# A two-stage expert layer around a recurrence: logits products of 128 columns, and a new plan

## Chip, cores and metric

One Trainium2 chip, one of its cores. The metric is the device time of one execution in microseconds, the median of the runs. All arithmetic is 32-bit floating point. A matrix product of this type is issued as two passes of TensorE, each with its own load of the stationary operand. The counts in the views are of such passes.

## What is computed

The reference, cut to its core, on 16 sequences of 512 tokens of 128 channels:

```python
def ffn(x, router_w, fc, proj):            # 8 experts, hidden width 512
    expert = argmax(softmax(x @ router_w.T))        # one expert for each token
    h = square(relu(x @ fc[expert]))
    return h @ proj[expert].T
x = x + 0.5 * ffn(layernorm(x))
x = x + rnn(layernorm(x))        # h = tanh(x @ Wi.T + bi + h @ Wh.T + bh), 512 steps
x = x + 0.5 * ffn(layernorm(x))
```

The 512 steps of the recurrence are one after the other. All 16 sequences move together, so a step's product moves 16 columns.

## The kernel before, in words

**Units, routes, tiles.** Time is cut into 16 units of 32 steps. A unit is 512 tokens, that is four blocks of 128 rows. A layer of experts handles its tokens in *routes*. The first layer has three, of 4, 4 and 8 units (FIRST, line 25), the second has seven (SECOND, line 28). For a route the kernel decides each token's expert. Blocks are transposed (`turn`), multiplied with the router's weights (`logits`, lines 1637 to 1647), the largest logit is taken (`pick`), a prefix count over the tokens gives each one's rank within its expert (`rank`), and `place` turns that into a row of a DRAM buffer sorted by expert. GpSimd (POOL in the views) then scatters the route's normalised rows, one indirect DMA for each block of 128. `head` and `entry` (first layer) or `list` (second) work out which sorted rows make a *tile*. A tile is 128 rows of one expert: 85 tiles in the first layer, 71 in the second.

**Stages.** A tile of the first layer may hold tokens of several units. A route's tile list is cut into stages (STEP, line 26, in units). Unit u of a route is complete when the tiles up to the end of its stage plus 7 more (one less than the experts) are stored (`needed`, lines 78 to 80). Route 1 (units 4 to 7) has STEP 3. Its first stage ends after 12 blocks, so unit 4 is complete with its 19th tile. Then POOL gathers the unit's four blocks back (`gather`, line 1197), VectorE (DVE) adds them, the unit is normalised (for a group of MIDDLE, line 27, together), transposed and multiplied with Wi, and its 32 steps can run.

**Beats.** TensorE (PE), VectorE and ScalarE (ACT) work in beats of one tile each. In a beat the next tile is transposed (`turn_x`, line 1684), the present one gets its first product (`product1`, 8 passes, line 1695), the one before its second (`product2`, 8 passes, line 1705). DVE does the relu of the present tile (line 1375) and finishes the last (lines 1382, 1385). ACT squares (line 1513) and copies the next tile's expert weights (line 1504), whose place it reads from the loaded tile. Some four steps of the recurrence (line 1715) lie between the products. Smaller pieces (decisions, statistics, transposes, logits) are put into beats as well. On DVE they come behind the relu and the finish (`b.dve`), or ahead of the relu (`b.front`). In the kernel before, `front` is only for the work of a recurrence unit that is soon due (`hurry`, line 713).

**Who sets the order.** Each engine's queue is an order written out ahead by `plan` (lines 147 to 810), a planner in Python. It plays all engines forward with constants for every duration and picks by urgency, with weights from PR (line 42). It has a model of TensorE's clock in `matmuls` (lines 367 to 379). Where the clock would fall it can put in idle products (`fill`, lines 404 to 409, emitted by `warm_up`, line 1722), in the kernel before only until the first tile is ordered. `keep_warm` (line 1718) issues two passes of 256 columns, in a beat that has steps but no tile.

**Queues.** POOL does the scatters (lines 1178, 1183), the gathers (1197), the output scatters of the second layer (`put`, 1203) and the reciprocal roots. Between indirect DMAs that come close together the planner puts a `rest`, a memset of 600 columns (line 1166), so that they follow each other at PACE 1.75 us. The sync engine's queue (SP) does the loads of tiles in order (line 1067 in the second layer) and the stores. A tile's load waits until the buffer of 12 tiles before is free, which in the second layer means that tile's put has landed. When the last route is counted, SP writes eight blank tiles behind the experts' rows (`close`, line 1080). The last 18 of the 71 tiles can be loaded only behind the last unit's four scatters.

**Start.** `first_in` (lines 127 to 139) orders the input loads: rows of units 0 to 3, zeros of the first buffer, then the rows of units 4 to 7 around the projection and fc weights, by AHEAD (line 50).

The product in question:

```python
j = 4 * i + q
mm = pe.matmul(lg[:, j * E:(j + 1) * E], xrt[:, m % XRING, q * P:(q + 1) * P], rwT, start=True, stop=True)
```

## Time and profile before

| | |
|---|---|
| median of 3 runs | 580.89 us (580.31 to 581.51) |
| profiled execution | 578.79 us |
| its span, first to last instruction | 576.4 us |
| mean granted TensorE clock | 0.950 |
| busy: PE, PE weight loads | 532.8 us (92%), 520.4 us (90%) |
| busy: DVE, ACT, POOL | 405.9 us, 315.4 us, 450.0 us |
| idle memsets on POOL (line 1166) | 141.8 us, 229 of them |

The profiled execution took 2.1 us less than the median, and 2.4 us of it lie outside the span. Busy shares are averages over stages with different limits, so the time is read by stage: a start up to the first tile's load, a stretch of tiles alone, the recurrence with tiles between its steps, and a tail behind the last step. A granted clock of 1.00 is 2.4 GHz, 0.50 is 1.2 GHz. DVE durations that overlap by some 0.1 us belong to a pipeline.

### The profile page before, as it was taken

How to read it: one execution, taken by the hardware profiler on the slowest of the kernel's cores; microseconds unless marked ns; L12 is line 12 of the kernel's file. 1: busy time of each engine (PE TensorE's matmuls, PEld its weight loads, DVE VectorE, ACT ScalarE, POOL GpSimd, SP SyncE). 2: the span in 40 equal slices, each digit the busy share in tenths (PEclk: the TensorE clock that was granted, in tenths of full speed). 3: DMA queues.
4: the chain of work that ended last, by engine and by line, in shares of the span. 5: the costliest groups of instructions: out<-in, count | busy, mean ns of one | idle time of the engine just before them, and what ended most of it. 6: DMA issues, size and time to landing. Idle time of an engine off the chain costs nothing.

```text
span 576.4 us, 15923 instructions
## 1 busy us (share of the span) xinstructions
PE 532.8 (92%) x4541; PEld 520.4 (90%) x4541; DVE 405.9 (70%) x1485; ACT 315.4 (55%) x1104; POOL 450.0 (78%) x562
## 2 busy tenths in 40 slices
PE   6849998899999999999999999999999999988991
PEld 6848997899999999999999999999999999877991
DVE  4799486778686798697569865777586467784650
ACT  2222363556666666566665666666656665544560
POOL 2497887559898887088997989978998938899982
PEclk8666599999999999999999999999999999999996
DMA  7974822222222232133323333322332301435410
GB/s 246 274 267 167 253 89 69 74 67 74 75 68 86 73 79 62 39 93 108 93 65 79 106 110 100 91 61 75 93 103 80 108 20 70 144 125 143 115 40 0
DMA packets 54147, 58.88 MB, mean 102 GB/s; under 512 B 8983, under 2 KB 42018, under 8 KB 54064
## 3 DMA queue, kind: packets, MB, share of 16 engines
q1 hardware_dynamic: 43776, 36.15, 21.4%
q0 software_dynamic: 9440, 21.06, 11.6%
q8 instruction: 40, 0.66, 0.5%
q10 hardware_dynamic: 848, 0.66, 0.5%
q14 instruction: 43, 0.35, 0.2%
HBM read 27.67 MB, written 30.62 MB: 101 GB/s over the span
## 4 chain that ended last, share of the span: by engine, by line
PE 71%; POOL 8%; DVE 8%; issue 5%; DMA 3%; SPq 1%; ACT 1%; POOLq 0%; ACTq 0%; DVEq 0%
PE yp L1705 23%; PE hp L1695 22%; PE z L1715 11%; PE mT L1601 4%; PE xTp L1684 4%; POOL idle L1166 3%; POOL xy_dram L1183 3%; PE lg L1645 3%; PE z L1665 2%; POOL out_dram L1203 2%; DMA hsT<-in_L_attn_x_dram 2%; ACT s_sb L1513 1%; PE hp L1720 1%; DVE pay L1252 1%; DVE r_sb L1375 1%
## 5 line engine op out<-in xcount | busy, mean ns | idle before, releaser
L1705 PE MATMUL yp<-projT,s_sb 128*128 x1248 | 204.0, 292 | 8.5 <-ACT s_sb L1513 8.2
L1695 PE MATMUL hp<-xT_sb,w_sb 128*128 128x128 f32 x1248 | 200.7, 289 | 0.3 <-ACT w_sb L1504 0.2
L1705 PEld LDWEIGHTS yp<-projT,s_sb 128*128 128x128 f32 x1248 | 164.1, 193 | 10.9 <-issue 10.8
L1695 PEld LDWEIGHTS hp<-xT_sb,w_sb 128*128 128x128 f32 x1248 | 166.0, 196 | 1.7 <-issue 0.5
L1484 ACT ACTIVATE hsT<-z 128x16 f32<-128x16 f32 x512 | 93.7, 183 | 134.1 <-PE z L1715 124.4
L1715 PE MATMUL z<-hsT,wT 128*128 128x16 f32 x1024 | 156.7, 229 | 0.1
L1715 PEld LDWEIGHTS z<-hsT,wT 128*128 128x128 f32 x1024 | 153.7, 190 | 3.2 <-ACT hsT L1484 0.3
L1513 ACT ACTIVATE s_sb<-r_sb 128x256 f32<-128x256 f32 (+1 forms) x260 | 114.2, 452 | 63.0 <-DVE r_sb L1375 31.6
L1375 DVE TENSOR_SCALAR r_sb<-hp 128x512 f32<-128x512 f32 x156 | 106.9, 685 | 56.9 <-PE hp L1695 54.8
L1166 POOL MEMSET idle<- 128x600 f32 x229 | 141.8, 619 | 0.2
L1504 ACT ACTIVATE w_sb<-fc_sb 128x256 f32 (+1 forms) x259 | 112.8, 455 | 4.6 <-issue 2.2
L1197 POOL DMA_INDIRECT back<-xy_dram,pos x64 | 62.9, 983 | 45.5 <-issue 37.9
L1203 POOL DMA_INDIRECT out_dram<-y_sb,xs_sb x71 | 70.7, 996 | 23.7 <-issue 14.0
L1183 POOL DMA_INDIRECT xy_dram<-pay,pos x64 | 63.3, 988 | 21.2 <-issue 10.2
L1178 POOL DMA_INDIRECT xs_dram<-pay,pos x64 | 62.9, 983 | 13.3 <-issue 10.4
L1369 DVE COPY xT_sb<-xTp 128x128 f32<-128x128 f32 x143 | 43.9, 307 | 12.8 <-PE xTp L1684 10.8
L1684 PE MATMUL xTp<-ident,xs_sb 128*128 128x128 f32 x156 | 47.0, 301 | 5.7 <-DVE xT_sb L1369 3.1
L1385 DVE TENSOR_SCALAR y_sb<-yp 128x128 f32<-128x128 f32 x85 | 24.5, 288 | 31.9 <-PE yp L1705 31.2
L1382 DVE SCALAR_TENSOR_TENSOR y_sb<-yp,xs_sb 128x128 f32<-128x128 f32 x71 | 20.6, 290 | 34.8 <-PE yp L1705 32.8
L1252 DVE TENSOR_SCALAR pay<-pay,mv,rstd 128x128 f32<-128x128 f32 x128 | 44.6, 488 | 0.4 <-POOL rstd L1156 0.4
L1645 PE MATMUL lg<-wT,xrt 128*128 128x8 f32 x256 | 41.0, 279 | 0.6 <-DVE pos L1298 0.3
L1156 POOL TENSOR_TENSOR rstd<-veps,half 128x4 f32<-128x4 f32 (+4 forms) x23 | 39.9, 1734 | 1.9
(133 smaller groups left out, 502.4 us busy)
## 6 DMA issues: line engine op xcount, KB each, us to landing
xs_sb<-xs_dram SPq DMA_DIRECT2D x71, 129.0 KB, 2.2
xy_dram<-zeros SPq DMA_DIRECT2D x11, 512.0 KB, 5.1
xs_sb<-xy_dram SPq DMA_DIRECT2D x85, 64.0 KB, 1.9
xy_dram<-y_sb SPq DMA_DIRECT2D x85, 64.0 KB, 1.6
hsT<-in_L_attn_x_dram SPq DMA_DIRECT2D x14, 256.0 KB
hsT<-n_L_ffn_expert_proj_dram SPq DMA_DIRECT2D x2, 1024.0 KB, 16.3
fc_sb<-in_L_ffn_expert_fc_dram SPq DMA_DIRECT2D x1, 2048.0 KB
out_dram<-y_sb,xs_sb POOLq DMA_INDIRECT x71, 2.6
```

What stands on the lines that cost most here:

```text
L1166: pool.memset(idle[:, :], 0.0).then_inc(s_idle, 1)
L1178: pool.indirect_dma_start(out=xs2_dram, in_=pay[:, n, :], in_offset=None, out_offset=bass.IndirectOffsetOnAxis(ap=pos[:, 1, n:n + 1].bitca ...
L1183: pool.indirect_dma_start(out=xy1_dram[r.index], in_=pay[:, n, XN:XN + D], in_offset=None, out_offset=bass.IndirectOffsetOnAxis(ap=pos[:, ...
L1203: pool.indirect_dma_start(out=out.rearrange("b t d -> (b t) d"), in_=y_sb[:, g % RING, :], in_offset=None, out_offset=bass.IndirectOffsetO ...
L1375: dve.tensor_scalar(r_sb[:, g % 2, :], hp[:, g % 2, :], 0.0, None, ALU.max).then_inc(s_relu, 1)
L1484: act.activation(state(t), z_step(t), ACT.Tanh).then_inc(s_h, 1)
L1504: act.activation(w_sb[:, g % 2, half * w:(half + n) * w], fc_sb[:, bass.ds(offsets[g] + half * w, n * w)], ACT.Copy).then_inc(s_wst, n)
L1513: act.activation(s_sb[:, g % 2, half * w:(half + n) * w, :].rearrange("p c t -> p (c t)"), r_sb[:, g % 2, half * w * P:(half + n) * w * P] ...
L1684: pe.transpose(xTp[:, 0:P], xs_sb[:, g % RING, XN:XN + D], ident[:, :]).then_inc(s_tx, 1)
L1695: mm = pe.matmul(hp[:, g % 2, h * P:(h + 1) * P], w_sb[:, g % 2, h * P:(h + 1) * P], xT_sb[:, g % 2, :], start=True, stop=True)
L1705: mm = pe.matmul(yp[:, 0:D], s_sb[:, g % 2, h, :], projT[:, bass.ds(offsets[g] + h * D, D)], start=(h == 0), stop=(h == HC - 1))
L1715: pe.matmul(z_step(t), WhT, state(t - 1) if t else hsT[:, 0:B], start=False, stop=True, skip_group_check=True).then_inc(s_mm, 1)
```

## The change

Six things are edited.

1. **Logits.** The router's weights get 120 columns of zeros behind their 8, set by one more memset on POOL. Each logits product moves 128 columns (fewer where the bank ends) and writes its 8 logits and zeros behind them, which the next product overwrites.
2. **The planner's clock.** Its model counts moved columns alone. Logits count as 128. `fill` works until the first tile's beats, measured from the end of PE's last real work (`worked`).
3. **The last route's decisions** may go to `front`, ahead of the relu.
4. **The puts.** None is planned from the last route's pick (less 2.011 us) until its scatters are ordered (`keep`), and behind them puts have no rests.
5. **Sizes.** Route 1 has STEP 2, so its first stage ends after 8 blocks and unit 4 is complete with its 15th tile. Units 11 to 14 are grouped as 1 and 3, where they were 2 and 2 with neighbours. Of the input rows, unit 6 is loaded earlier and unit 7 later, behind fc.
6. **PR.** New values throughout, so the order on every engine is new.

```diff
-STEP = [1, 3, 1]
-MIDDLE = [1, 1, 1, 1, 1, 1, 1, 1, 1, 2, 2, 2, 1]
+STEP = [1, 2, 1]
+MIDDLE = [1, 1, 1, 1, 1, 1, 1, 1, 1, 2, 1, 3, 1]
...
-AHEAD = [2, 4, 7]
+AHEAD = [3, 3, 6]
...
-            p = min((p for p in pool_wait if p[0] <= start), key=pool_urgency)
+            if ("pick", second[-1]) in ev and second[-1] not in sorted_out:
+                soon = [p for p in pool_wait if p[1][0] != "put" or max(pool_free, p[0]) < ev["pick", second[-1]] + PR["keep"]]
+                start = max(pool_free, min([p[0] for p in soon], default=limit))
+                if start >= limit:
+                    return
+            else:
+                soon = pool_wait
+            p = min((p for p in soon if p[0] <= start), key=pool_urgency)
...
-                while REST and drained > start + PR["burst"]:
+                while REST and drained > start + PR["burst"] and not (what == "put" and second[-1] in sorted_out):
...
-                clock = 0.5 if moved < 12 and clock == 1.0 else 1.0 if busy > 0.95 * WINDOW else clock
-                begun, busy, moved = begun + WINDOW, 0.0, 0.0
+                clock = 0.5 if moved < ACTIVE else 1.0
+                begun, moved = begun + WINDOW, 0.0
...
-                n = int((need[0] - pe) / 0.25) if not order else 0
+                n = int((max(need[0], pe) - worked) / 0.25) if len(order) <= 1 else 0
                 if n > 0:
                     b.idle[place] = n
+                    pe = worked
                     matmuls(2 * n, 128, 0.0)
...
-                hurry = isinstance(job[0], Middle) and (job[0].u0 * UNIT - t) * 0.66 < PR["crit"]
+                hurry = (job[0].u0 * UNIT - t) * 0.66 < PR["crit"] if isinstance(job[0], Middle) else job[0] and job[0].second and job[0].last and PR["end"] > 0
...
-        wT = sb("wT", [P, 2 * P + E])
+        wT = sb("wT", [P, 3 * P])
...
+            pool.memset(wT[:, 2 * P + E:], 0.0).then_inc(s_const, 1)
...
                 for q in (2 * half, 2 * half + 1):
-                    j = 4 * i + q
-                    mm = pe.matmul(lg[:, j * E:(j + 1) * E], xrt[:, m % XRING, q * P:(q + 1) * P], rwT, start=True, stop=True)
+                    at = (4 * i + q) * E
+                    n = min(P, 512 - at)
+                    mm = pe.matmul(lg[:, at:at + n], xrt[:, m % XRING, q * P:(q + 1) * P], wT[:, 2 * P:2 * P + n], start=True, stop=True)
```

## Rows read from the trace of the kernel before

**Rows 1.** The page, part 2: busy tenths and granted clock in 40 slices.

```profile
PE   6849998899999999999999999999999999988991
...
PEclk8666599999999999999999999999999999999996
```

**Rows 2.** The chain that ended last, in order of time: start, length, what.

```profile
54.23 1.78 DMA xs_sb<-xy_dram
```

**Rows 3.** Stretches of PE: length, busy (passes), granted clock, DMA share, GB/s.

```profile
49.00:52.00 3.00, 3.00 (x16) 0.50 0.47 167
...
56.00:72.13 16.13, 15.83 (x74) 0.50 0.79 250
```

**Rows 4.** PE's groups in 49 to 55 us, then in 20.7 to 24.3 us.

```profile
L1645 PE MATMUL lg<-wT,xrt 128*128 128x8 f32 x22 | 4.9, 348 | 0.0
L1601 PE MATMUL mT<-ident,hsT 128*128 128x128 f32 x8 | 2.2, 429 | 0.0
...
L1725 PE MATMUL yp<-ident 128*128 128x128 f32 x8 | 1.9, 421 | 0.0
```

**Rows 5.** Timeline of PE: last logits before the first tile; later two beats' second products.

```profile
53.42 1.71 PE L1645 MATMUL lg<-wT,xrt 128*128 128x8 f32 x8
...
542.96 1.06 PE L1705 MATMUL yp<-projT,s_sb 128*128 x8
...
544.85 1.06 PE L1705 MATMUL yp<-projT,s_sb 128*128 x8
```

**Rows 6.** Timeline of the start: route 0's logits, normalisation, pick, first scatter; route 1's rank.

```profile
14.30 3.42 PE L1645 MATMUL lg<-wT,xrt 128*128 128x8 f32 x16
...
16.88 1.12 DVE L1252 TENSOR_SCALAR pay<-hsT,mv,rstd 128x128 f32<-128x128 f32 x4 [3.51 <-POOL rstd L1156]
17.91 0.28 DVE L1259 TENSOR_REDUCE best<-lg 128x16 f32<-128x128 f32 x1
...
24.13 1.23 POOL L1183 DMA_INDIRECT xy_dram<-pay,pos  x1 [7.29 <-DVE pos L1298]
...
41.57 0.29 PE L1653 MATMUL lg<-oh,before 128*128 128x128 bf16 x1 [7.96 <-DVE oh L1263]
```

**Rows 7.** The steps as a whole; unit 4's last tile, its gather, the steps around.

```profile
L1715 PE MATMUL z<-hsT,wT x1024: 179/262/283, 116.7 to 495.7; 128*128 128x16 f32 x171
...
191.76 0.29 DVE L1385 TENSOR_SCALAR y_sb<-yp 128x128 f32<-128x128 f32 x1
...
194.92 1.00 POOL L1197 DMA_INDIRECT back<-xy_dram,pos  x1 [1.70 <-issue]
...
207.48 0.29 PE L1715 MATMUL z<-hsT,wT 128*128 128x16 f32 x2
...
215.80 0.29 PE L1715 MATMUL z<-hsT,wT 128*128 128x16 f32 x2
```

**Rows 8.** keep_warm's stretch (L1720 alone), then all engines: PE, PEld, DVE, ACT, POOL.

```profile
485.00:497.00 12.00, 6.61 (x20) 3.07 (x20) 1.00 0.35 105
...
497.00:523.00 26.00, 20.98 (x179) 19.85 (x177) 18.72 (x64) 12.66 (x24) 23.55 (x30) 1.00 0.45 134
523.00:533.00 10.00, 8.87 (x74) 8.46 (x75) 4.88 (x13) 5.13 (x9) 9.01 (x12) 1.00 0.53 147
```

**Rows 9.** Timeline of the last unit's decision: DVE, then POOL.

```profile
506.02 0.18 DVE L1259 TENSOR_REDUCE best<-lg 128x4 f32<-128x32 f32 x1
...
510.63 0.29 DVE L1298 TENSOR_SCALAR pos<-posf 128x4 int32<-128x4 f32 x1
...
511.05 0.97 POOL L1203 DMA_INDIRECT out_dram<-y_sb,xs_sb  x1 [0.17 <-issue]
...
512.80 0.97 POOL L1178 DMA_INDIRECT xs_dram<-pay,pos  x1 [0.17 <-issue]
```

**Rows 10.** Timeline of the end: DVE's last result, POOL's last put.

```profile
564.79 0.29 DVE L1382 SCALAR_TENSOR_TENSOR y_sb<-yp,xs_sb 128x128 f32<-128x128 f32 x1 [1.50 <-PE yp L1705]
...
565.88 0.97 POOL L1203 DMA_INDIRECT out_dram<-y_sb,xs_sb  x1 [0.20 <-issue]
```

More of the change, by code:

```diff
@@ L41 @@
 JMAX = UR * max(FIRST + MIDDLE + SECOND)
[L42 to L47 removed]
+PR = {'proj': -47.746, 'lat1': 14.303, 'lat2': 5.889, 'lat3': -50.516, 'last': -221.946,
+      'hor': 129.448, 'beat': 9.17, 'put': -26.524, 'dve': 2.201, 'act': 2.925, 'pe': 2.195,
+      'early': 0.409, 'load': 2.441, 'hold': -40.798, 'slack': 191.806, 'near': 0.051,
+      'tol': 0.107, 'mix': -11.014, 'late': 6.755, 'root': -17.056, 'gather': -114.978,
+      'scatter1': -67.157, 'scatter2': 5.337, 'crit': 18.341, 'front': 7.019, 'dvx': 0.781,
+      'burst': 0.3, 'keep': -2.011, 'end': 1.531}
 TURNS = ("turn", "turn2", "hadd")
 EARLY = 8
[L50 removed]
+AHEAD = [3, 3, 6]
 FORCED = ("x", "b0", "c0", "d0")
@@ L214, in plan @@
     turns_of, logits_of, est, held = [], [], {}, []
-    clock, begun, busy, moved = 1.0, 0.0, 0.0, 0.0
+    clock, begun, moved, worked = 1.0, 0.0, 0.0, 5.0
     def ahead_of(r):
@@ L367, in matmuls @@
     def matmuls(n, columns, need):
-        nonlocal pe, clock, begun, busy, moved
+        nonlocal pe, clock, begun, moved, worked
         at = max(pe, need)
@@ L427, in split @@
                 if p[0] == "logits":
[L428 removed]
+                    return passes(place, 4, 128, (("turn", p[1], p[2]), lg_after[p[1].index]), p if half else None)
                 return passes(place, 4, 128, (("turn2", p[1]), ("h", UNIT * (p[1] - 1) - 1) if p[1] >= 2 else None), p if half else None)
```

20 lines of the change are left out of this document (7 added, 13 removed).

## The prediction

> **What bounds the kernel now.** I read the page's slices first, then the chain, then each stretch by itself. TensorE is busy in nearly every slice from the second sixth to the end, but its granted clock is low in slices 2 to 5 [rows 1]. So two things cost time: stretches in which PE works at 1.2 GHz, and the few in which it idles. The chain names where the first tile comes from: its load lands at about 56.0 us [rows 2]. Ahead of that PE's clock costs little, because the wait is for route 0's scatters. From there to 72.13 PE is busy 15.83 of 16.13 us at clock 0.50 [rows 3]. That stretch is on the path: behind it tiles and steps queue for PE until the last tile. At full clock a beat of a tile alone takes 544.85 - 542.96 = 1.89 us for 17 passes, 0.111 us each [rows 5]. In the slow stretch a pass takes 15.83 / 74 = 0.214 us [rows 3].
>
> The recurrence runs from 116.7 to 495.7 us [rows 7], 0.742 us a step over 511 intervals, with PE full in the slices [rows 1]. So it shares a bound with the tiles. Only at two places does one stand without the other: no step starts for 8.32 us at unit 4 [rows 7], while tiles run on, and in 485 to 497 us there is no tile to go with the steps and keep_warm runs idle products [rows 8]. In the tail PE idles 26.00 - 20.98 = 5.0 us up to 523 and 1.1 us up to 533 [rows 8]. Then beats follow at 1.89 us to the end.
>
> **The parts of the change.** *Wider logits, their direct price.* In the low clock the 22 logits passes and 8 transposes of 128 columns fill 49 to 55 us, and the mean durations differ by 429 - 348 = 81 ns [rows 4]. That is their length, not their spacing: of 49 to 52 us they take 3.00 for 16 passes, 0.19 us each, against 0.214 in the stretch that is mostly 128 columns [rows 3]. The price is between 0 and 0.03 us a pass at low clock. It is nearest 0, because the weight loads are unchanged. At full clock a 128-column pass takes 0.111 us [rows 5], and no row times a run of 8-column ones, so the bound is 0.111 at most for each of the 128 passes after 72 us (half of 256), 14 us. I take 0, since a step's 16-column pass is 262 ns long in the median against 1.06 us for eight 128-column ones that still start 0.111 apart [rows 5, 7]: the width hides in the pipeline. A gain from width alone is excluded, since nothing is left out.
>
> *Wider logits, the clock.* In 49 to 52 us PE is 3.00 of 3.00 us busy and the clock is 0.50 [rows 3]. Three quarters of the passes are 8 columns wide [rows 4]. The clock was back at 24.3 us behind a stretch with eight idle products of the identity and transposes [rows 1, 4]. So busy time is not what lifts it. Moved columns fit, and columns that are nearly all zero (the identity's) seem to count. With 128 columns for each logits pass I expect full clock from about 43 us on, and `fill` to hold it over the 0.9 us before 56.0. The 74 passes then need 74 x 0.111 = 8.2 us, not 15.83: 7.6 less. Half of the shorter stretch's pieces hang on DVE and ACT. If PE idles there as much as in the tail's 26 us, 5.0 of 26 [rows 8], the stretch lasts 8.2 / 0.81 = 10.1 and 5.7 are gained. I take 7.0. The ends are 0 and 7.9 (with the 0.3 of idle).
>
> A rule of the Trainium skill speaks against this part. "TensorE: Matmul & The Clock Gate", Part 1, says that the clock depends on how busy the engine has been, and gives full clock after a sustained busy stretch. By that rule wider logits change nothing. Rows 3 do not agree: fully busy, and 0.50.
>
> *The start.* Route 0's last 16 logits passes take 3.42 us from 14.30, and its pick starts at 17.91, its first scatter at 24.13 [rows 6]. At full clock these passes take 1.8 us. Then the pick could start 1.6 us sooner. DVE's normalisation stands from 16.88 to 18.00 [rows 6], and the new order can put it behind. The bound is 0 to 2.5 us (another 0.9 if the rank's passes, too, run at full clock). I take 1.5. POOL's added memset stands ahead of the constants that PE and DVE wait for: under 0.62 us by the 600-column memset of the table, 0.1 taken, inside this term. Unit 7's rows come behind fc now. What covers it is DVE: PE waited 7.96 us for DVE's pick of route 1, not for rows [rows 6]. If that cover went, route 1's scatters would be late, and next its tiles, which are due only when route 0's 23 are done.
>
> *STEP 2.* The gather of unit 4 starts at 194.92, 3.16 us behind the 19th tile's result at 191.76 [rows 7]. Four tiles fewer, each in a beat of some four steps (4 x 0.742 = 3.0 us), put it some 12 us sooner, and more than the stall is covered. The recurrence gains 8.32 - 0.74 = 7.6 us. PE does not, because it worked on tiles there. POOL has four gathers to do inside route 2's scatters, so these end 4 x 1.75 = 7.0 us later: late next would be route 2's first tiles. The regrouped units change no count of roots or pieces, and one DVE instruction of `place` goes: 0.
>
> *What the freed recurrence is worth.* With the last step 7.6 sooner, keep_warm's stretch goes. Its 20 passes of 256 columns are worth some 20 x 0.22 = 4.4 us of tiles. The tail's 6.1 us of idle shrink if more tiles are left to cover the last decision. Together 10.5 us at most, 0 at least; below zero if the new order makes idle of its own, as much as the tail's 5.0. I take 4.5, under half, since POOL is 78% busy, and nearly full in the late slices' rows (23.55 of 26 us) [rows 8], so it gives no free hand.
>
> *The last decision.* Its pick starts at 506.02 behind a relu and a finish, its positions end at 510.92, but POOL is in a put from 511.05 and scatters at 512.80 [rows 9]. Ahead of the relu the pick can start up to 1.7 us sooner, and without the put the scatter starts 1.75 sooner. This lies on the recurrence's path: steps, decision, scatter, last 18 tiles. PE's own path is the longer one as long as it has tiles, so I count 0.5. Bounds are -1 and 3.4. The negative end is a held put: its buffer is waited for by the load 12 tiles on, that load stands ahead of the rest on SP, and PE waits for it.
>
> *No rests in the tail.* The last result is ready at 565.08, and the last put starts at 565.88, behind a rest [rows 10]. It could start at 565.25: 0.6 us. Before that tiles come at 1.89 us, slower than the pace of 1.75, so rests cost nothing else.
>
> Sum: 7.0 + 1.5 + 4.5 + 0.5 + 0.6 = 14.1 us. From the profiled execution's 578.8 that gives 564.7. The median lay 2.1 higher, so 566.8. I say 566.5.
>
> **The rivals.** *All idle recovered.* The plan was written for a clock that the chip did not grant from 43 to 72 us. One that is right there may also remove the small stalls: 7.9 + 2.5 + 10.5 + 1 + 0.6 = 22.5, so 558.4. For it speaks that PE is the only bound in most slices. Against it stands POOL's load.
>
> *Only the clock's part.* PE gains 7 us and the new order loses what it recovers: 580.9 - 7.0 - 0.6 = 573.3. For it speaks that idle in the tail comes from DVE and SP chains that a sum of PE time does not show.
>
> *Columns don't set the clock.* Something else in these passes keeps it low, or zeros don't count. Then the change does not do what it says, and only the plan's parts remain: 580.9 - 4.5 - 0.6 = 575.8. This is also what the busy-time rule above would give. Rows 3 and 4 speak against it.
>
> *Slower: fill at half clock.* The place is the wait for the first tile. PE's real work ended there at about 55.1 [rows 5]. A plan that believes in full clock has it end near 50 and puts (56.0 - 50) / 0.25 = 24 idle products, 48 passes, behind it. At 0.50 they last 48 x 0.214 = 10.3 us from 55.1, to 65.4: the first tile is 9.4 late. The rest gains 0.6 and perhaps 3: 580.9 + 9.4 - 3.6 = 586.7. It decides from the point where the clock at 50 us is 0.50 and idle passes number more than (0.9 + 3.6) / 0.214 = 21. The clock's fall and rise in slices 2 to 5 [rows 1] speak for it a little. The identity's columns speak against it.
>
> **Chances.** My forecast (562 to 571) 0.52, all recovered 0.20, clock alone 0.16, columns don't count 0.05, slower by fill 0.04, no change at all 0.03. The likeliest case's time is the prediction, 566.5. The range takes in the first three cases and most of their bounds: 556 to 576. A measurement of this kernel can tell about 0.2% (1.2 us) from no change. Faster by more has 0.93, within it 0.03, slower 0.04.
>
> **What would show it.** Clock 1.00 from about 43 to 72 us, and the first tile's beats at about 1.9 us from 56. First scatter at 22 to 23 us. The first step at 107 to 110, and no gap of several us at step 128. Fewer than 20 idle passes of 256 columns. PE's idle between the last step and the last scatter's load below 5 us. The last put 0.2 us behind the last result. It would be wrong if the clock is 0.50 at 60 us with 128-column logits, if a new gap stands in the steps at unit 8 or later (route 2's tiles late), or if the tail's idle grows.

## The result, and the profile after

The changed kernel is slower by about half a percent. Over 16 runs its median is 583.29 us, against 581.31 us for 16 runs of the kernel before beside it; the ratio is 1.0053, 95% interval [1.0028, 1.0078]. A second set on another chip gave 1.0078 [1.0041, 1.0114]. The forecast was 566.5 us in a range of 556 to 576. The granted clock differs from execution to execution: fourteen of the changed kernel's runs go from 580.3 us at a mean clock of 0.988 to 588.1 at 0.971, and two slow ones, which no ratio counts, took 592.1 and 594.6 us at 0.961 and 0.958. So single profiles are compared by their parts, and the ratios carry the verdicts.

The page of the changed kernel, part 2, against [rows 1], and its stretches of PE against [rows 3] (length, busy and passes, clock, DMA share, GB/s):

```profile
PE   7899988899899999999999999999999999769991
...
PEclk9999999999999999999999999999999999979997
```

```profile
49.00:52.00 3.00, 3.00 (x28) 1.00 0.60 225
56.00:72.13 16.13, 15.03 (x123) 1.00 0.76 230
```

The clock is at 1.00 through the whole start, where it was 0.50 in both stretches. In the same 3 us PE gets 28 passes done instead of 16. In the other row, besides a fuller third slice, two slices near the end are at 7 and 6 tenths where there were 9 and 8.

The start, on GpSimd (first scatters of route 0), and the last logits before the first tile, against [rows 5, 6]:

```profile
20.13 1.24 POOL L1193 DMA_INDIRECT xy_dram<-pay,pos  x1 [3.60 <-DVE pos L1308]
...
32.22 0.96 POOL L1193 DMA_INDIRECT xy_dram<-pay,pos  x1 [5.60 <-DVE pay L1262]
```

```profile
54.66 2.01 PE L1657 MATMUL lg<-wT,xrt 128*128 128x128 f32 x16
56.50 1.50 PE L1737 MATMUL yp<-ident 128*128 128x128 f32 x12
```

The first scatter is 4.0 us earlier than in [rows 6], and the gain is gone twelve us later: the fifth scatter waits 5.60 us for VectorE's normalised rows and starts at 32.22, where it started at 31.40 before.

The steps (TensorE's instructions of the recurrence, first and last start), and the steps around unit 4, against [rows 7]:

```profile
L1727 PE MATMUL z<-hsT,wT x1024: 182/262/374, 114.1 to 492.6; 128*128 128x16 f32 x171
```

```profile
208.23 0.29 PE L1727 MATMUL z<-hsT,wT 128*128 128x16 f32 x2
212.57 0.29 PE L1727 MATMUL z<-hsT,wT 128*128 128x16 f32 x2
```

The stall at unit 4 is 4.34 us instead of 8.32, yet the last step is only some 3 us earlier.

The stretch from the last step on, all engines (PE, PEld, DVE, ACT, POOL), against [rows 8]:

```profile
497.00:523.00 26.00, 17.40 (x122) 16.43 (x123) 13.58 (x47) 9.12 (x18) 19.79 (x23) 0.87 0.41 115
523.00:533.00 10.00, 10.00 (x92) 10.00 (x91) 6.01 (x16) 5.76 (x10) 4.93 (x6) 1.00 0.54 146
```

PE idles 8.6 of the first 26 us instead of 5.0, and does 122 passes instead of 179, because the clock also falls: it is 0.50 from 506.5 to 509.9 and from 513.3 to 516.7. Here the time went. GpSimd, then VectorE and one row of ScalarE in that stretch, against [rows 9] (only the rows that matter; "remote" is a count that arrived later than any record of the work that raises it):

```profile
499.64 1.00 POOL L1213 DMA_INDIRECT out_dram<-y_sb,xs_sb  x1 [0.30 <-issue]
500.94 0.99 POOL L1213 DMA_INDIRECT out_dram<-y_sb,xs_sb  x1 [0.30 <-issue]
...
508.10 0.99 POOL L1188 DMA_INDIRECT xs_dram<-pay,pos  x1 [0.35 <-issue]
...
514.66 1.00 POOL L1213 DMA_INDIRECT out_dram<-y_sb,xs_sb  x1 [0.30 <-issue]
515.96 0.99 POOL L1213 DMA_INDIRECT out_dram<-y_sb,xs_sb  x1 [0.30 <-issue]
```

```profile
505.48 0.29 DVE L1392 SCALAR_TENSOR_TENSOR y_sb<-yp,xs_sb 128x128 f32<-128x128 f32 x1 [1.80 <-remote]
505.59 0.28 ACT L1530 ACTIVATE xT_sb<-xTp 128x128 f32<-128x128 f32 x1 [1.19 <-remote]
506.56 0.56 DVE L1308 TENSOR_SCALAR pos<-posf 128x4 int32<-128x4 f32 x1
...
520.59 0.29 DVE L1392 SCALAR_TENSOR_TENSOR y_sb<-yp,xs_sb 128x128 f32<-128x128 f32 x1 [3.88 <-remote]
```

The last decision is indeed earlier: scatters from 508.10, against 512.80. But puts stand 1.30 us apart on both sides of it, and VectorE twice waits for TensorE's semaphores, although the matmuls that raise them (yp from 500.68, in 8 passes of 0.11 us) are long recorded as done. VectorE's instruction at 520.59 also waits for the put of the tile 12 before it, whose output buffer it reuses, but that put's count had stood since 470.9 us. In the trace's records of the semaphores only TensorE's counts are late. Four pieces of its work, recorded as ended at 501.74, 501.95, 502.11 and 503.04 us, are counted at 505.46, 505.53, 505.56 and 505.65. Most counts come 0.01 us behind the recorded end. The last of the four has eight passes of 0.11 us in it, 0.9 us of work, and its count stands 0.09 us behind the one before. So this work had been done, and its counts came late. For the first of the four alone that is not settled.

The end, against [rows 10]:

```profile
567.78 0.29 DVE L1392 SCALAR_TENSOR_TENSOR y_sb<-yp,xs_sb 128x128 f32<-128x128 f32 x1 [1.49 <-PE yp L1717]
```

```profile
568.88 0.98 POOL L1213 DMA_INDIRECT out_dram<-y_sb,xs_sb  x1 [0.55 <-issue]
```

The last result is 2.99 us later than before, and the last put still stands 1.10 us behind it (start to start), without a rest.

**One table for all runs.** I cut each profiled execution at two events: the first step and the last step (ScalarE's tanh), and measured on to VectorE's last result. The three lengths sum to the time of the last result.

| kernel | first step | steps | last step to last result |
|---|---|---|---|
| before | 117.0 | 379.3 | 68.4 |
| changed | 114.5 | 378.5 | 74.9 |
| changed, second profile (e20) | 114.5 | 377.1 | 75.3 |
| e1 wide logits alone | 113.1 | 381.1 | 69.6 |
| e2 change, rests back | 114.3 | 381.2 | 71.0 |
| e3 change, decision behind relu | 115.3 | 378.1 | 76.3 |
| e5 before, no rests past the last scatter | 111.4 | 380.5 | 73.2 |
| e6 change, old constants | 114.7 | 392.7 | 68.7 |
| e7 e2 with idle passes at tile 37 | 114.4 | 382.2 | 71.5 |
| e8 e2 with the list behind relu | 113.3 | 377.8 | 72.6 |
| e10 change, rests back ahead only | 115.1 | 379.9 | 76.0 |
| e11 change, short rests | 113.4 | 376.7 | 69.9 |
| e12 e1, places early | 112.6 | 380.4 | 69.7 |
| e13 e1, 12 scatters bare | 111.9 | 378.8 | 68.2 |
| e14 change, rests back behind only | 113.4 | 384.3 | 69.9 |
| e15 e1, all scatters bare | 109.0 | 378.0 | 68.7 |
| e16 e1, puts bare in the middle | 112.5 | 379.3 | 70.7 |
| e17 e1, five puts bare | 113.0 | 381.0 | 69.0 |
| e18 e1, no rests past the last scatter | 111.1 | 381.4 | 73.9 |
| e19 e5 again | 113.9 | 381.0 | 73.4 |

Before, e5 and e19 run one program up to the last scatter, and their first steps lie at 117.0, 111.4 and 113.9. So a difference of 3 us in the first column of two single profiles shows nothing. Nor is the clock at the start the same in the three. The half-clock stretch that ends at 72.1 us in the kernel before ends at 61.8 in e5 and at 62.1 in e19. Their rows for the stretch that [rows 3] give with 74 passes at 0.50 (e5, then e19):

```profile
56.00:72.13 16.13, 16.05 (x117) 0.82 0.88 266
56.00:72.13 16.13, 16.04 (x114) 0.81 0.85 262
```

The third column sets the change off clearly: 74.9 and 75.3 against 68.4. It has its own scatter, from execution to execution and chip to chip. Five profiles have before's tail unchanged (before, e1, e13, e15, e16) and go from 68.2 to 70.7, mean 69.1. The same tail without rests behind the last scatter (e5, e18, e19) has 73.2 to 73.9, mean 73.5. The change's tail with rests behind the last scatter (e2, e7, e11, e14) has 69.9 to 71.5, mean 70.6, and without them (the change twice, e10) 74.9 to 76.0, mean 75.4. So the rests are worth 4.4 and 4.8 us of this column, beyond the scatter. The change's order costs 1.5 and 1.9 on the means, which is within it or near.

### The profile page after: what moved, and what is told of

Its sections match the earlier page's. It is cut to its first block, busy times and chain, and to the rows that moved or that the text cites. A ratio compares the mean times of both kernels' runs of the same rounds, so it can differ in the third digit from the quotient of the medians.

```text
span 579.0 us, 16141 instructions
## 1 busy us (share of the span) xinstructions
PE 536.5 (93%) x4665; PEld 522.6 (90%) x4665; DVE 403.6 (70%) x1474; ACT 318.2 (55%) x1111; POOL 434.9 (75%) x538
## 4 chain that ended last, share of the span: by engine, by line
PE 71%; DVE 11%; issue 5%; POOL 4%; DMA 3%; SPq 2%; another core or an unknown queue 1%; ACT 0%; POOLq 0%; ACTq 0%; DVEq 0%
PE yp L1717 24%; PE hp L1707 22%; PE z L1727 12%; PE mT L1611 4%; PE xTp L1696 4%; PE z L1677 3%; PE lg L1657 3%; POOL xy_dram L1193 2%; DVE pay L1262 2%; DMA hsT<-in_L_attn_x_dram 1%; POOL idle L1176 1%; DVE r_sb L1385 1%; DVE stats L1252 1%; SPq L1046 1%
## 5 line engine op out<-in xcount | busy, mean ns | idle before, releaser
L1176 POOL MEMSET idle<- 128x600 f32 x204 | 126.7, 621 | 0.4
L1514 ACT ACTIVATE w_sb<-fc_sb 128x256 f32 (+1 forms) x257 | 113.1, 458 | 4.6 <-issue 1.6
L1379 DVE COPY xT_sb<-xTp 128x128 f32<-128x128 f32 x133 | 39.6, 298 | 9.6 <-PE xTp L1696 5.4
L1262 DVE TENSOR_SCALAR pay<-pay,mv,rstd 128x128 f32<-128x128 f32 x128 | 45.9, 509 | 0.0
L1657 PE MATMUL lg<-wT,xrt 128*128 128x128 f32 x256 | 38.5, 285 | 0.2 <-ACT xrt L1544 0.2
```

What stands on the lines that cost most here:

```text
L1176: pool.memset(idle[:, :], 0.0).then_inc(s_idle, 1)
L1514: act.activation(w_sb[:, g % 2, half * w:(half + n) * w], fc_sb[:, bass.ds(offsets[g] + half * w, n * w)], ACT.Copy).then_inc(s_wst, n)
```

## The experiments

All ratios are against the kernel before on the same chip. The experiments ran in five groups, each on a chip of its own: e1 to e5, e6 to e10, e11 to e14, e15 to e17, e18 to e20. So medians in us are compared within a group only, and ratios of different groups with both intervals.

**e1: the wide logits alone.**

```
 before
-    mm = pe.matmul(lg[:, j*E:(j+1)*E], xrt[...], rwT, ...)
+    at = (4 * i + q) * E
+    n = min(P, 512 - at)
+    mm = pe.matmul(lg[:, at:at + n], xrt[...], wT[:, 2*P:2*P + n], ...)
 (and the zeros of wT with the counts of s_const)
```

> The kernel before with one part of the change alone: the logits' products are 128 columns wide (the zeros of the weight tile and their memset with them); plan, order, rests and decisions stay as before. Theory A (the columns set the clock, and the step pipeline turns the clock into time): granted clock 1.00 in most of 0 to 75 us and mean clock above 0.97, first y some 5 us earlier, and the end 3 to 8 us earlier than before (573 to 578 against 581). Theory B (the early lead is lost later whatever the plan, because loads, GpSimd and the routes' stalls set the middle and the tail): the same clock and first y, but the end within 1.5 us of before. Theory C (the columns do not set the clock): clock 0.50 for 16 of the first 72 us as before, and no change.

Measured: ratio 0.9970 [0.9946, 0.9994], 577.69 us against 579.76. Its page and its stretches:

```profile
PEclk9878999899999999999999999999999999999996
```

```profile
49.00:52.00 3.00, 3.00 (x28) 1.00 0.46 169
56.00:72.13 16.13, 16.04 (x124) 0.89 0.88 264
```

The width of the logits does change the clock: beside one memset nothing else changed, and the clock at 49 to 52 us is 1.00, in all six profiles with this start, against 0.50 in all three with narrow logits. The mean clock is 0.973 against 0.954. But the end comes only 2.1 us earlier (of a forecast term of 7.0), between theories A and B. Its six profiles (e1, e12, e13, e16 to e18, all with this start) have the first step at 111.1 to 113.1, mean 112.4; the three with narrow logits have a mean of 114.1. The first tile is finished at 64.2 instead of 68.5, but e5 and e19, with narrow logits, finish it at 64.9. Against them the lead is 0.7 us, and PE does 124 passes from 56.00 to 72.13 where they do 117 and 114. So most of the term of 7.0 us was the long half-clock stretch of one execution. In the two others PE did 28 and 29 passes at 0.50 from 56.0 to 61.8 us, 5.8 us that would take 3.1 to 3.2 at 0.111 us a pass. That leaves an estimate of 2.6 to 2.7 us to gain, near e1's 2.1.

**e2, e3: the tail of the changed kernel, rests and decision.**

```
 e2: change
+ from 16 entries ahead of the last scatter on: one rest ahead of each put
+ that follows a put or a scatter; several rests in a row become one
 e3: change
+ for b in beats:
+     late = [p for p in b.front if len(p) > 1 and getattr(p[1], "last", False)]
+     b.front = [p for p in b.front if p not in late]
+     b.dve = late + b.dve
```

> The changed kernel, same order, with one rest of 0.48 us put back before each put or scatter's successor in the stretch from 16 entries ahead of the last scatter to the end, and the group of 5 rests there cut to 1. Theory T1 (puts at 1.30 us back to back hold up the counting up of semaphores by TensorE, which stops the steps twice for 2 to 4 us after 499 and 515): the waits of VectorE on y_sb at about 505.5 and 520.6 go, the clock stays at 1.00 past 500, tiles are 4 to 7 us earlier at 521, and the end is 3 to 6 us earlier than the changed kernel (577 to 580). Rival (the wait is VectorE's or ScalarE's own order and the late semaphores are a fault of the record): the two stops stay and the time is within 1 us of the changed kernel, or later by the rests.

> The changed kernel with the pieces of the last route's decision moved from ahead of relu to behind it in their beats; nothing else moves. Theory T2 (place and list ahead of relu at 505.7 to 511.1 cost the steps one wait of ScalarE of 5.2 us, of which some 3 us reach the end): the end 1.5 to 3.5 us earlier than the changed kernel. Rival (they pay by an earlier last gather and last tiles): the end 1 us or more later. Third: within 0.5 us, because the steps stand on the late semaphores in both.

Measured: e2 1.0009 [0.9979, 1.0039], e3 1.0110 [1.0051, 1.0169]. e2 has no late count, 71.0 us in the last stretch against 74.9. So T1 holds in its waits: with the rests back the last stretch is 3.9 us shorter. The ratio is lower by 0.0044 than the change's 1.0053, and by 0.0069 than e20's, both on other chips. The intervals reach 0.0025 to 0.0037 to a side, and those of the first pair overlap. T1 missed in its clock, which did not stay at 1.00. PE waits for s_sb behind the early decision, and the clock is 0.50 from 512.4 to 519.3 us in e2:

```profile
513.11 2.07 PE L1726 MATMUL yp<-projT,s_sb 128*128 x8 [3.67 <-ACT s_sb L1532]
```

The stretch is 2.5 us longer than in the kernel before's profile. T2 falls. Behind relu the decision makes the tail no shorter, and the ratio is higher than the change's, though the intervals overlap. PE's waits in e3 hint at what the early decision buys:

```profile
513.62 1.63 PE L1721 MATMUL yp<-projT,s_sb 128*128 x8 [3.44 <-ACT s_sb L1527]
520.25 0.48 PE L1700 MATMUL xTp<-ident,xs_sb 128*128 128x128 f32 x1 [5.00 <-DMA xs_sb<-xs_dram]
```

The wait for s_sb is there all the same (3.01 in the change), and behind it PE waits 5.00 us for a load of the sorted rows. The last four scatters start 1.0 us later than in the change (509.12 against 508.10) and are counted as landed 1.6 us later (518.57 against 517.00).

**e5, and again e19: the kernel before without rests past the last scatter.**

```
 before
+ last = max(n for n, w in enumerate(pool_order) if w[0] == "scatter" and w[1].last)
+ pool_order = [w for n, w in enumerate(pool_order) if n < last or w[0] != "rest"]
```

> The kernel before with every rest behind the last scatter left out (puts back to back to the end) and nothing else changed. Theory T1: puts at 1.30 us one behind the other hold up TensorE's semaphores wherever they stand: waits of VectorE or ScalarE on TensorE's results of 2 us and more show up between 515 and 540, and the time rises by 1 to 6 us over before. Rival (as the change's words have it, rests past the last scatter only cost time): the last put comes earlier by up to 0.6 us, the time falls by 0 to 0.6 us.

> The kernel before without rests behind the last scatter, the same program as in the first call, beside the two others. If the harm belongs to the program: 1.006 to 1.012 of before again. If it hangs on the chip or on the moment of the execution: 0.998 to 1.003, or times in two groups.

Measured: 1.0091 [1.0056, 1.0127], and on another chip 1.0081 [1.0050, 1.0112]. By the ratios that is 5.3 and 4.7 us. Last stretch 73.2 and 73.4 us against 68.4. So the loss belongs to the program, not to the chip, and leaving the rests out costs the kernel before at least what the whole change costs.

**e10, e14: which row of puts.**

```
 e10: e2's rule only up to the last scatter      e14: only behind it
```

> The changed kernel with rests put back only for the four puts ahead of the last scatters (499.6 to 503.5) and the group of 5 rests cut to 1; the puts behind the last scatter stay back to back. Theory T1a (the burst ahead of the scatters, which the planner's rule takes in beside what the change names, does the harm): within 1 us of the kernel with all rests back, 579 to 580.5. Theory T1b (the burst behind the last scatter does it): the time stays at the changed kernel's 582 to 584 and a wait on late semaphores shows at 515 to 520. Both: in between, about 581 to 582.

> The changed kernel with rests put back only behind the last scatter; the four puts ahead of the last scatters stay back to back, the group of 5 rests stays. Together with the kernel that has them back only ahead (76.0 us from the last step to the last y) and the one that has all back (71.0) this splits the loss. If the burst behind the scatters does nearly all: 71 to 72.5 us, time 579 to 581. If each does its own harm (two stops of TensorE's semaphores, 505.5 and 520.6): the first stop stays, 73 to 75 us, 581 to 583.

Measured: e10 1.0026 [0.9986, 1.0066] with 76.0 us in the last stretch; e14 1.0030 [0.9995, 1.0066] with 69.9. The ratios cannot part the two, and e14's steps took 384.3 us in its profile at a clock that fell twice. The last stretch can: the row behind the last scatter does the harm (T1b). In e14 the four puts ahead of the scatters are as close as in the change, and VectorE waits there for no late count (the first two):

```profile
504.52 1.00 POOL L1225 DMA_INDIRECT out_dram<-y_sb,xs_sb  x1 [0.30 <-issue]
505.82 0.99 POOL L1225 DMA_INDIRECT out_dram<-y_sb,xs_sb  x1 [0.30 <-issue]
```

I had expected 73 to 75 us if each row did its own harm, and that is not what happened. But the change has late counts at the first row too (505.48), which the row behind it cannot have caused, and e14, with the same order there, has none. So one and the same first row has late counts in three profiles (the change twice, e3) and none in e14, and what differs in e14 stands further back in the queue.

**e11: short rests.**

```
 e2, but the rests put back are
+ pool.memset(idle[:, 0:200], 0.0)        (600 columns elsewhere)
```

> The changed kernel in the order of the second kernel tried, but between the puts around and past the last scatters stands a memset of 200 columns instead of 600, so that they follow each other at about 1.45 us instead of 1.30 or 1.78. Theory T1 with a queue that fills (each transfer costs more to carry out than 1.45 us, the lag adds up over a row of puts): the stretch from the last step to the last y is between 71.0 (full rests) and 74.9 us (none), waits on late semaphores of 1 us and more still show behind the last scatter, and the time lies between 579.7 and 583.3. Theory T1 with a threshold just above 1.30: no late semaphores, 71 us and 578.5 to 580.

Measured: 1.0009 [0.9975, 1.0042], no late count, 69.9 us. The puts stand 1.43 to 1.45 us apart:

```profile
511.20 0.99 POOL L1222 DMA_INDIRECT out_dram<-y_sb,xs_sb  x1 [0.17 <-issue]
512.17 0.30 POOL L1185 MEMSET idle<- 128x200 f32 x1
512.64 0.98 POOL L1222 DMA_INDIRECT out_dram<-y_sb,xs_sb  x1 [0.17 <-issue]
```

A rest of a third of the length does the same as a full one. This speaks against the queue that fills. A threshold of spacing alone is not the rule either, since e14 above and e16 and e17 below have puts 1.28 to 1.30 us apart and no late count.

**e13, e15, e16: rows without rests elsewhere.**

```
 e13: e1 without the rests inside the 12 scatters in a row at the routes' middle
 e15: e1 without any rest between two scatters of a route (the last route keeps its own)
 e16: e1 without the rests between puts 96 and 107
```

> The kernel before with the wide logits, and in the middle of the run, where 12 scatters stand in a row with a rest between each two, these rests left out (one stays behind the last of them); all else as in the first kernel tried (577.7). Theory T1 (indirect transfers issued without a rest hold up the counting up of semaphores wherever they stand): waits of VectorE or ScalarE on TensorE's results, or of TensorE on theirs, that show as late semaphores of 2 us and more within 25 us of the burst, the steps 2 to 6 us later behind it, the end 2 to 6 us later. Rival (only puts past the last scatter do it, because of what they write): no late semaphores, and the time within 1 us of 577.7 or earlier, since the scatters land 5 us sooner.

> The kernel before with the wide logits, and no rest between any two scatters of a route that follow each other (the last route's four keep theirs); rests stay around gathers and puts. If scatters without rests are harmless, as the 12 of them in the middle were (no late semaphore, ratio 0.9966): no late semaphore anywhere, the routes' rows land earlier, 0.994 to 0.998 of before. If that one stretch was an exception: late semaphores of 1 us and more at another row of scatters, the steps later from there, 1.000 to 1.01 of before.

> The kernel before with the wide logits, and no rest between the 12 puts 96 to 107, in the middle of the steps, which the 12 scatters ahead of them have piled up; all else as in the first kernel tried. Theory Q (it is the kind of transfer: a put, which reads a tile in two places and writes rows of the output, holds up the semaphores where scatters don't): late semaphores of 2 us and more within 15 us behind the row of puts, near 395 to 415, the steps 2 to 5 us later from there, 1.002 to 1.007 of before. Theory R (it takes what stands only behind the last scatter, a row of tile loads by the sync engine at the same time, 200 GB/s): no late semaphore, 0.995 to 0.998 as with the wide logits alone.

Measured: e13 0.9966 [0.9942, 0.9989], e15 0.9910 [0.9879, 0.9941], e16 0.9991 [0.9964, 1.0017]. No late count in any of them. So puts or scatters close to each other don't hold up semaphores by that alone. e16's ratio lies between what the two theories gave (1.002 to 1.007, 0.995 to 0.998), and without late counts it speaks for R, whose row of loads was not tested by itself. In e16 the puts stand as close as in the change:

```profile
412.20 0.97 POOL L1207 DMA_INDIRECT out_dram<-y_sb,xs_sb  x1 [0.30 <-issue]
413.48 0.97 POOL L1207 DMA_INDIRECT out_dram<-y_sb,xs_sb  x1 [0.30 <-issue]
```

e15 beats both kernels and its own forecast of 0.994 to 0.998: 570.70 us against 576.57. Its scatters of route 0 follow each other at 1.27 us, where rests make it 1.75 (22.17 to 23.91 in the changed kernel), the first tile's result comes at 62.1 us against 68.5 before (64.9 in e5 and e19), and the first step at 109.0:

```profile
25.49 0.97 POOL L1190 DMA_INDIRECT xy_dram<-pay,pos  x1 [0.30 <-issue]
26.77 0.96 POOL L1190 DMA_INDIRECT xy_dram<-pay,pos  x1 [0.31 <-issue]
```

**e17, e18: five puts, or all.**

```
 e17: e1 without rests in the 10 entries behind the last scatter (5 puts)
 e18: e1 with e5's edit
```

> The kernel before with the wide logits, and no rests between the first five puts behind the last scatter (129 to 133); from there on rests as before. In the kernel before without any rests there the semaphores came 3.4 and 5.2 us late at 519 and 522, that is within these first puts. If the harm is made there: late semaphores of 2 us and more at 515 to 523, the stretch from the last step to the last y 72 to 74 us against 69.6, ratio 1.003 to 1.008 of before. If it takes the long row: no late semaphore, 69 to 70 us, 0.995 to 0.999.

> The kernel before with the wide logits and with every rest behind the last scatter left out. If the row of puts without rests costs what it cost the kernel before (1.0091 against 1.000, with semaphores 3.4 and 5.2 us late): 1.004 to 1.009 of before, 72 to 75 us from the last step to the last y. If it is the first five puts alone that can do harm and they did none here (0.9985): 0.996 to 1.000. The puts from the sixth on follow the tiles at 1.9 us anyway, so the two programs differ in nothing that can be seen.

Measured: e17 0.9985 [0.9957, 1.0013], e18 1.0036 [1.0011, 1.0061]. The two have the same order on GpSimd up to the fifth put behind the last scatter, at the same spacing, and then the puts of both follow the tiles. Yet VectorE's waits differ from the third put on. e18, GpSimd and then VectorE:

```profile
515.42 0.99 POOL L1206 DMA_INDIRECT out_dram<-y_sb,xs_sb  x1 [0.30 <-issue]
516.71 0.98 POOL L1206 DMA_INDIRECT out_dram<-y_sb,xs_sb  x1 [0.30 <-issue]
518.00 0.97 POOL L1206 DMA_INDIRECT out_dram<-y_sb,xs_sb  x1 [0.31 <-issue]
```

```profile
518.43 0.69 DVE L1378 TENSOR_SCALAR r_sb<-hp 128x512 f32<-128x512 f32 x1 [2.44 <-remote]
522.72 0.29 DVE L1385 SCALAR_TENSOR_TENSOR y_sb<-yp,xs_sb 128x128 f32<-128x128 f32 x1 [3.60 <-remote]
```

e17, the same two engines:

```profile
516.91 0.99 POOL L1207 DMA_INDIRECT out_dram<-y_sb,xs_sb  x1 [0.30 <-issue]
518.20 0.98 POOL L1207 DMA_INDIRECT out_dram<-y_sb,xs_sb  x1 [0.30 <-issue]
519.48 0.97 POOL L1207 DMA_INDIRECT out_dram<-y_sb,xs_sb  x1 [0.30 <-DVE y_sb L1386]
```

Not one wait on a late count stands in e17's profile. What differs up to that moment is only what stands further back in the queues. I can't say why that matters. e17 has one profile, so luck of that execution is not excluded, but its ratio over 12 runs shows no loss like e18's.

**e20: the change again, beside e18 and e19.** No edit.

> The changed kernel itself, beside the same runs of the kernel before, as the measure for the two others. If the loss belongs to the program: 1.003 to 1.008 again, with late semaphores at about 505 and 520 us. If it hangs on the chip or the moment: within 0.2% of before, and no late semaphores in its profile.

Measured: 1.0078 [1.0041, 1.0114], late counts at 503.17, 504.62 and 519.76 us. The loss and its places repeat.

**e6: old constants in the new program.**

```
 change
- PR, STEP = [1, 2, 1], MIDDLE, AHEAD = [3, 3, 6] of the change
+ PR, STEP = [1, 3, 1], MIDDLE, AHEAD = [2, 4, 7] of before; no 'keep', no 'end'
- and not (what == "put" and second[-1] in sorted_out)
```

> The changed kernel's program with the planner's constants of before (costs, STEP, MIDDLE, AHEAD), no puts kept back around the last pick, rests between puts past the last scatter as before, decisions not ahead of relu in the last units; what stays of the change is the wide logits and the planner that costs them and fills idle stretches with passes by its new count. Theory P (the new constants of the plan make the loss in 150 to 220 us and the tail): no half-clock stretch at 155 to 165, and about the time of the wide logits alone, 576 to 579 against 580. Rival (the planner's new picture of clock and fill makes the loss, whatever the constants): half-clock stretches past 100 us as in the changed kernel, and 580 to 584.

Measured: 1.0146 [1.0091, 1.0201]. Theory P falls. The half-clock stretches past 100 us that the rival named are there, but its 580 to 584 us was too low: 589.03. The steps take 392.7 us, with three new gaps between steps of 2.9 to 4.0 us, and a clock of 0.74 from 320 to 340:

```profile
320.00:340.00 20.00, 19.97 (x133) 0.74 0.34 102
```

The constants belong to the picture of costs for which they were found. That says nothing of which new constant costs what, and I did not try them one by one.

**e7, e8, e12: mending the change.**

```
 e7: e2, and ahead of the turn of tile 37
+    for _ in range(12):
+        pe.matmul(hp[:, now % 2, 0:P], ident[:, :], ident[:, :], start=True, stop=True)
 e8: e2 with the two list pieces of the last route moved from b.front to b.dve
 e12: e1 with "place" of the last route in b.front, and put 128 behind the last scatters
```

> The changed kernel with a rest between puts around and past the last scatters, as in the second kernel tried, and 12 passes of 128 columns on the identity put into TensorE's queue ahead of the turn of tile 37, where TensorE stood idle for 1.5 us at 156 to 158 while VectorE made a route's list (their result is overwritten and never read). Theory F (that idle stretch lets the clock fall to 0.50 behind it, 3 to 4 us lost in every execution and more in some): granted clock 1.00 from 150 to 175 us, the end 3 to 4 us earlier than the same kernel without the passes (576 to 577 against 579.7), and less scatter between executions. Rival (the clock falls for another reason, such as work before that point): the stretch stays and the time is the same or later by up to 1 us.

> The changed kernel with a rest between puts around and past the last scatters, and of the last route's decision only the places stay ahead of relu; the two pieces that make its list (4 us of VectorE, 507.4 to 511.7 in the second kernel tried) go behind relu and the finish of their beats. Theory L (the places ahead of relu bring the last scatters forward and are worth their time; the list ahead of relu is pure loss, because the loads that need it stand on the scatters' landing after 517): the wait of TensorE on s_sb of 3.7 us at 513 shrinks to under 1.5, the last loads come no later, and the end is 1 to 3 us earlier than 579.7. Rival (the recurrence's loads set the end in both): no change within 0.5 us.

> The kernel before with the wide logits and with two edits in its last decision: its places stand ahead of relu in their beat, and one put (128) goes behind the last four scatters instead of ahead of them; rests stay everywhere. In the first kernel tried the last scatters started at 510.3, 1.6 us behind the places, and the next tile's load came 2.4 us late at 522. Expected if these scatters set the end: last scatter 1.5 to 2.4 us earlier, the wait on the load under 1 us, the end 1 to 2 us earlier than 577.7 (575.5 to 577). Rival (the held put delays a store slot or relu's delay costs as much): 577.5 to 579.

Measured: e7 0.9984 [0.9944, 1.0024], e8 1.0063 [1.0027, 1.0099], e12 0.9992 [0.9965, 1.0020]. e7's fill did what it should where it stands. The stretch from 150 to 175 us, first in the changed kernel, then in e2, then in e7:

```profile
150.00:175.00 25.00, 22.84 (x188) 0.93 0.22 66
```

```profile
150.00:175.00 25.00, 23.50 (x154) 0.73 0.21 62
```

```profile
150.00:175.00 25.00, 24.33 (x216) 1.00 0.23 70
```

Eight profiles have this order and no fill there (the change twice, e2, e3, e8, e10, e11, e14). Seven of them show a clock under 1.00 in this stretch, and e8, whose profile is the fastest of its 12 runs, does not. The time at 0.50 is 3.4 us in the change (twice), e3 and e11, and 6.9 to 13.7 in e14, e10 and e2. PE had stood idle there (changed kernel):

```profile
157.90 0.30 PE L1696 MATMUL xTp<-ident,xs_sb 128*128 128x128 f32 x1 [1.49 <-DVE xT_sb L1379]
```

VectorE was making a route's list until 157.46. In e7 the steps behind this place run 4.2 us ahead of e2's, which has the longest of these stretches. Then another stretch at low clock between 350 and 400 us (0.90) took it all back, and the interval holds both 0 and a gain: theory F is right for the place, and open for the time. e8 missed: the last stretch grew to 72.6 us. e12 missed too (575.5 to 577 against 577.7 had been expected, that is 0.993 to 0.995 of before): its last scatter came 20.0 us behind the last step instead of 21.4, and the last stretch stayed at 69.7 us.

## Why the prediction was wrong

**The wide logits and the clock: right in mechanism, mis-sized.** The clock was 1.00 from 49 to 72 us as forecast. In e1, which changes the width alone, PE is 3.00 of 3.00 us busy at 1.00 where it was as busy at 0.50. The busy-time rule of the Trainium skill, "TensorE: Matmul & The Clock Gate", Part 1, does not agree with that. Two terms were mis-sized. The first is the 7.0 us. It took the 16 us at half clock of one execution for the program's, and in the two other profiles of the same start (e5, e19) full clock was back at 61.8 and 62.1 us. The step behind it, "that stretch is on the path: behind it tiles and steps queue for PE", then passed on even less: e1 measured 2.1 us in all (0.3%). The second is the direct price of the width, taken as 0. At full clock four narrow passes hold the next work back by 0.37 us (kernel before), and four wide ones by 0.45 (changed kernel):

```profile
501.98 0.51 PE L1645 MATMUL lg<-wT,xrt 128*128 128x8 f32 x4
502.35 1.14 PE L1705 MATMUL yp<-projT,s_sb 128*128 x8
```

```profile
497.89 0.61 PE L1657 MATMUL lg<-wT,xrt 128*128 128x128 f32 x4
498.34 1.06 PE L1717 MATMUL yp<-projT,s_sb 128*128 x8
```

That is 0.02 us a pass, and up to 2.6 us over the 128 passes behind 72 us, an estimate that takes PE for the bound there. In the changed kernel not even that arrived: nine executions of its start have the first step at 113.3 to 115.3, mean 114.2, against 114.1 for the three of before's.

**The start: wrong.** The first scatter came 4.0 us earlier, more than the bound of 2.5, but I carried the term to the end of the route without asking what the fifth scatter waits for. It waits 5.60 us for the normalisation, which the new order had put back.

**STEP 2 and the freed recurrence: wrong in size.** I expected the stall of unit 4 to go (7.6 us) and took 4.5 as its worth. It shrank to 4.34. The steps as a whole took 378.5 and 377.1 us in the change's two profiles, but 376.7 to 384.3, mean 379.2, in the eight that share its order up to the last step (e2, e3, e8, e10, e11 and e14 too), against 379.3 to 381.0, mean 380.3, in the three of before's. So 1 us is left, less than the scatter. The new order lost part of it to a stretch at half clock behind an idle of 1.49 us. My condition "below zero if the new order makes idle of its own" named this, but I priced idle by its length alone, not by the clock that follows. The longest of these stretches (13.7 us, e2) cost 4.2 us against e7. In the change it was 3.4 us long: from the first step to step 96 the change takes 71.4 us, and e8, without such a stretch, 69.8.

**The last decision: sign wrong.** Scatters were earlier, as said: 20.5 us behind the last step at the last of them, not 21.7. But when the last unit's rows have landed, the next tile to be turned is number 133 in the change and 137 in the kernel before. The four tiles more that are left, at 1.89 us each, are worth 7.6 us, and the rows that land earlier take only part of that off. With all rests back the last stretch is 2.5 us longer than before's (e2), and 1.5 with short ones (e11). That is near the scatter of this column, so the sign rests on the tiles counted and on PE's waits: 1.80 and 3.67 us (e2) where the kernel before has 1.38 and 1.45. Which of the moved pieces costs it stays open, since neither e3 nor e8 made the tail shorter. I had written that PE's own path is the longer one, and did not count how many tiles were left on it.

**No rests: the step that failed most.** "Rests cost nothing else" took for granted that a rest only costs. Behind the last scatter it is worth more than it costs. Forecast 0.6 us gained; measured 0.9% and 0.8% lost on the kernel before (e5, e19: 5.3 and 4.7 us), and some 0.4% on the change (e2 against it, with intervals that overlap). What it does there was not found. The expected gain at the last put stayed away: it starts 1.10 us behind the start of the last result, as it did behind a rest (1.09), and 1.08 behind it in e5, where GpSimd stood idle for it. I had also read the rule as "past the last scatter", where the program takes rests from four puts ahead of it as well.

**The sum.** Against the kernel before's 564.8 us at the last result, the change's 567.8 is -2.5 at the first step, -0.9 in the steps and +6.4 behind them; of the 6.4, 3.9 go with the rests (e2) and 2.5 with the order. On the means of the table it is 4.8 and 1.5. The -2.5 is within what executions of one program differ by. No rival had this. The one on the slower side, 586.7, is nearest in number, but it named fill passes at half clock, which did not occur: the clock was 1.00 there, with 12 such passes. "Only the clock's part" came nearest in mechanism, and even that was 2.1 us and not 7. One sign that the prediction had named as its own refutation did show: the tail's idle grew.

## What to carry to other kernels

A pause that looks like pure cost may be paying for something; take pauses out at one kind of place at a time, and measure each. Here those between scatters were waste (e15, 0.9% gained, of which the wide logits alone give 0.3%) and those behind the last scatter were not (0.9% and 0.8% lost), though the trace of the kernel before shows no difference between them. And a stretch at half clock is worth what its lead still is at the next event that everything waits for: read the lead there, and the length of the stretch itself, over several executions, before it goes into a sum.

## What the runs showed of the hardware

With no rests behind the last scatter, TensorE's semaphores were seen raised late in bursts in the profiles of the change (twice), e5, e10, e18 and e19: VectorE waited 1.08 to 4.20 us at a time for counts whose matmuls were recorded as done. e3 has the same rows of puts. Its view calls no wait remote, but two counts come 0.91 and 1.47 us behind their work, at 502.20 and 503.66 us, and its last stretch is as long. Puts at 1.28 us in the middle (e16), scatters at 1.27 us anywhere (e13, e15), five puts at the same place followed by rests (e17), and rests of a third of the length (e11) show none. In these profiles nearly all counts of the tiles' matmuls are recorded (153 to 157 where 156 are due, for each semaphore). In e1, e2 and e8 a fifth to a third are missing, so "no late count" is weaker there. What holds the semaphores up stays open. The records of matmuls end where a model puts them, so the first matmul of a burst may itself have been late. Behind it the counts are what is late: eight passes that take 0.9 us are counted 0.09 to 0.10 us behind the work ahead of them (the change, e20, e10, e18, e19).

A stretch of logits passes of 128 columns, of which 120 are zero, ran at a clock of 1.00 (49 to 52 us in e1, 28 passes), where passes of 8 columns, just as busy, had 0.50 [rows 3]. At full clock a pass of 128 columns costs 0.02 us more than one of 8.

TensorE's clock is not the same in two executions of one program: the half-clock stretch that begins at 48 us ended at 72.1, 61.8 and 62.1 us in three of them.
